# An adaLN and mixture-of-experts kernel: four experts' rows go into cleared tables instead of being added in DRAM

## The reference, cut to what matters

```python
x = x + ga * causal_mean(layernorm(x) * (1 + ca) + sa)     # softmax of a causal mask: a running mean
h = layernorm(x) * (1 + cb) + sb                           # S rows of D
scores = softmax(h @ gate_weight.T).T                      # E x S
vals, idx = top_k(scores.reshape(-1), 2 * S)               # 8192 (expert, row) pairs over all experts
gate = zeros(E, S).at[expert, row].add(vals)
y = gelu(h @ W1[e] + b1[e]) @ W2[e] + b2[e]                # for the chosen rows of each expert
shared = gelu(h @ Ws1 + bs1) @ Ws2 + bs2                   # for all rows
out = x + gb * (sum over e of gate[e] * y[e] + shared)
```

## Time and profile before

| | |
|---|---|
| median of 3 runs | 344.6 us (342.89 to 345.53) |
| the profiled execution | 346.31 us |
| its span (first to last instruction) | 344.3 us |
| granted TensorE clock, mean | 0.909 of full speed |
| PE busy | 272.8 us (79%) |
| POOL busy | 209.4 us (61%) |
| DVE busy | 158.4 us (46%) |
| ACT busy | 139.1 us (40%) |
| mean DMA rate | 70 GB/s |

### The profile page before, as it was taken

The page is one execution under the profiler, slowest core; times in us unless marked ns, Lnnn a source line. Parts: engine busy times, 40 slices in busy tenths (PEclk is TensorE's granted clock), DMA queues, the critical chain, the costliest instruction groups (busy, mean ns, idle before and its releaser), DMA issues.

```text
span 344.3 us, 4085 instructions
## 1 busy us (share of the span) xinstructions
PE 272.8 (79%) x1033; PEld 144.6 (42%) x1033; DVE 158.4 (46%) x758; ACT 139.1 (40%) x238; POOL 209.4 (61%) x242
## 2 busy tenths in 40 slices
PE   5889778999998596878999999999975916777400
PEld 1757765343444253444454444444432303336200
DVE  2899865567655446363945556342222202211100
ACT  4659966354333312324444444445421302333100
POOL 5667841000037374463888888788888888788661
PEclk9999995899999988989999999999988785998955
DMA  7901220039102242221534353535343332233321
GB/s 207 340 8 33 61 64 0 30 99 224 1 13 84 65 118 61 75 76 53 100 37 104 40 100 41 108 31 101 41 102 40 46 38 32 47 47 39 37 23 12
DMA packets 26463, 23.93 MB, mean 70 GB/s; under 512 B 7224, under 2 KB 21375, under 8 KB 26432
## 3 DMA queue, kind: packets, MB, share of 16 engines
q0 software_dynamic: 11968, 9.23, 19.8%
q1 hardware_dynamic: 14338, 14.32, 14.6%
q10 hardware_dynamic: 126, 0.04, 0.0%
HBM read 14.23 MB, written 9.34 MB: 68 GB/s over the span
## 4 chain that ended last, share of the span: by engine, by line
POOL 43%; issue 20%; PE 19%; DMA 6%; DVE 5%; ACT 2%; POOLq 1%; DVEq 1%; SPq 0%
POOL out_dram L1092 27%; POOL R L1074 15%; PE U L1236 6%; PE Y L1278 5%; DMA out_dram<-YO,IDXB 5%; PE Y L1167 2%; PE R L1125 1%; DVE YO L923 1%; PE LG L1188 1%; DVE ST L560 1%; DMA XW<-in_L_attn_x_dram 1%; ACT H2F L400 1%; PE U L1125 1%; PE R1b L1125 1%; DVEq L920 1%
## 5 line engine op out<-in xcount | busy, mean ns | idle before, releaser
L1092 POOL DMA_INDIRECT out_dram<-YO,IDXB x68 | 107.6, 1583 | 30.5 <-issue 22.3
L1074 POOL DMA_INDIRECT R<-rows_scratch,IDXB x68 | 66.3, 975 | 74.6 <-DVE IDXB L879 55.1
L464 ACT ACTIVATE HF<-U,COL 128x512 f32<-128x512 f32 x96 | 65.9, 687 | 102.6 <-PE U L1243 45.4
L1243 PE MATMUL U<-XT,XW 128*128 128x512 f32 x128 | 69.0, 630 | 2.9 <-issue 2.9
L1282 PE MATMUL Y<-HF,XW 128*128 128x512 f32 x128 | 66.4, 611 | 0.0
L923 DVE SCALAR_TENSOR_TENSOR YO<-R1b,R,GBR 128x128 f32<-128x128 f32 x64 | 18.0, 344 | 92.3 <-DMA out_dram<-YO,IDXB 50.3
L1236 PE MATMUL U<-H2F,WS 128*128 128x512 f32 x64 | 38.9, 693 | 0.1
L1243 PEld LDWEIGHTS U<-XT,XW 128*128 128x128 f32 x128 | 24.6, 204 | 29.2 <-issue 25.8
L1278 PE MATMUL Y<-HF,WS 128*128 128x512 f32 x64 | 35.9, 644 | 0.0
L1282 PEld LDWEIGHTS Y<-HF,XW 128*128 128x128 f32 x128 | 23.0, 195 | 19.8 <-issue 19.8
L485 ACT ACTIVATE XT<-R 128x512 f32<-128x512 f32 x17 | 10.2, 597 | 41.8 <-PE R L1125 40.3
(11 more groups left out here) (214 smaller groups left out, 351.6 us busy)
## 6 DMA issues: line engine op xcount, KB each, us to landing
XW<-in_wx_dram SPq DMA_DIRECT2D x10, 512.0 KB, 5.6
XW<-in_L_attn_x_dram SPq DMA_DIRECT2D x8, 256.0 KB, 7.4
rows_scratch<-HT SPq DMA_DIRECT2D x8, 256.0 KB, 3.3
out_dram<-SHO SPq DMA_DIRECT2D x8, 256.0 KB
R<-rows_scratch,IDXB POOLq DMA_INDIRECT x68
out_dram<-YO,IDXB POOLq DMA_INDIRECT x68
INV<-in_inv_dram SPq DMA_DIRECT2D x3, 256.0 KB, 6.8
WS<-in_wsx_dram SPq DMA_DIRECT2D x1, 512.0 KB, 6.8
```

The source lines that it names most:

```text
L464: eng.activation(HF[:, g % RING, :], UB[g % 2][:, :], ACT.Gelu_apprx_tanh, bias=B1[:, at:at + 1]).then_inc(M["a_gelu"], 1)
L1074: eng.indirect_dma_start(XG[:, v % XR, s, :], None, rows_dram, bass.IndirectOffsetOnAxis(ap=IDXB[:, v, s:s + 1], axis=0)).then_inc(M[f"ld_ ...
L1092: eng.indirect_dma_start(out, bass.IndirectOffsetOnAxis(ap=IDXB[:, v, s:s + 1], axis=0), YO[:, v % 2, s, :], None, compute_op=ALU.add).the ...
L1243: eng.matmul(bank[:, :], weights(v, 0, c, 0), XT[:, v % 2, :], start=True, stop=True).then_inc(M["pe_up"], 1)
```

## The change

Experts 0 to 3 (NTAB = 4, units 0 to 7) no longer add to the output. Each has a table of its own in DRAM (`sums`, S + 512 rows of 128). SP clears the tables with 16 DMAs of 512 KB (`clear`), 5 of them between the stores of the normalised rows and 11 behind the store of the scores. The eight scatters of units 0 to 7 write to these tables without adding and without waiting for each other.

The shared part stays in SBUF, in `X2`: `close` adds in place and nothing is stored then. When both units of an expert e have landed, SP loads its table back in eight pieces of 256 KB (`load_sums`) through four buffers, `TB`, which take the place of `INV`. DVE adds each piece to `X2` (`add_sums`): four at c = 1 and four at c = 2 of unit 2e+5, so in units 5, 7, 9 and 11. Pieces 4 to 7 can be loaded only when the adds of pieces 0 to 3 have freed a buffer. After the last expert's adds SP stores the eight blocks (`store_base`); scatter 8 waits for these stores, and scatters 8 to 16 add as before.

`YO` gets four buffers, `XG` twelve in place of ten. `gathered` lets GpSimd issue all that is left of the gathers behind scatter 7: with 50 issued by then, 18 follow in one run.

```diff
-XR = 10
+XR = 12
+NTAB = 4
+YR = 4
+TBR = 4
@@ def gathered(v):
-    return min(max(NT * AHEAD + PER_GAP * (v + 1), NT * (v + 4)), NT * NMAIN)
+    if v >= 2 * NTAB - 1:
+        return NT * NMAIN
+    return max(NT * AHEAD + PER_GAP * (v + 1), NT * (v + 4))
@@
+    sums = [nc.dram_tensor(f"sums_scratch{e}", [S + NPAD, D], F32, kind="Internal").ap() for e in range(NTAB)]
+        TB = INV
-        SHO = sb("SHO", [P, 2, BLK])
-        YO = sb("YO", [P, 2, NT, P])
+        YO = sb("YO", [P, YR, NT, P])
@@ def sync(eng):
+            def clear(i):
+                e, q = i // NT, i % NT
+                n = NB * NT // NT
+                eng.dma_start(by_partition(sums[e])[:, q * n:(q + 1) * n, :].rearrange("p (a t) c -> p a (t c)", t=NT),
+                              ZERO[:, :].unsqueeze(1).to_broadcast([P, n // NT, BLK])).then_inc(M["st_tz"], 16)
+
+            def load_sums(e, b):
+                if b == 0:
+                    for v in (2 * e, 2 * e + 1):
+                        eng.wait_ge(M[f"st_sc{v % YR}"], 64 * (v // YR + 1))
+                if NB * e + b >= TBR:
+                    eng.wait_ge(M["v_add"], NB * e + b - TBR + 1)
+                else:
+                    eng.wait_ge(M["v_ct"], NB)
+                eng.dma_start(TB[:, b % TBR, :].rearrange("p (t c) -> p t c", t=NT),
+                              by_partition(sums[e])[:, b * NT:(b + 1) * NT, :]).then_inc(M[f"ld_tb{b % TBR}"], 16)
+
+            def store_base(b):
+                eng.wait_ge(M["v_add"], NB * (NTAB - 1) + b + 1)
+                eng.dma_start(by_partition(out)[:, b * NT:(b + 1) * NT, :],
+                              X2[:, b, :].rearrange("p (t c) -> p t c", t=NT)).then_inc(M["st_out"], 16)
+
             for b in range(NB):
                 eng.wait_ge(M["a_ht"], b + 1)
                 eng.dma_start(by_partition(rows_dram)[:, b * NT:(b + 1) * NT, 0:D],
                               HT[:, b % NHT, :].rearrange("p (t c) -> p t c", t=NT)).then_inc(M[f"st_ht{b % NHT}"], 16)
+                if b < NB - 3:
+                    clear(b)
@@
+            for i in range(NB - 3, NTAB * NT):
+                clear(i)
             for s in range(NSTEP):
-                if s in CLOSE_AT:
-                    b = CLOSE_AT[s]
-                    eng.wait_ge(M["v_out"], b + 1)
-                    eng.dma_start(by_partition(out)[:, b * NT:(b + 1) * NT, :],
-                                  SHO[:, b % 2, :].rearrange("p (t c) -> p t c",
-                                                             t=NT)).then_inc(M[f"st_out{b % 2}"], 16)
@@
+                if c == 3 and v >= 4 and v % 2 == 0 and v // 2 - 2 < NTAB:
+                    for b in range(TBR):
+                        load_sums(v // 2 - 2, b)
+                if c == 0 and v >= 5 and v % 2 and v // 2 - 2 < NTAB:
+                    for b in range(TBR, NB):
+                        load_sums(v // 2 - 2, b)
+                if c == 3 and v == 2 * NTAB + 3:
+                    for b in range(NB):
+                        store_base(b)
@@ def vector(eng):
-                if b >= 2:
-                    eng.wait_ge(M[f"st_out{b % 2}"], 16 * (b // 2))
-                eng.tensor_tensor(SHO[:, b % 2, :], RB[1][:, :], X2[:, b, :], ALU.add).then_inc(M["v_out"], 1)
+                eng.tensor_tensor(X2[:, b, :], RB[1][:, :], X2[:, b, :], ALU.add).then_inc(M["v_out"], 1)
+
+            def add_sums(e, b):
+                eng.wait_ge(M[f"ld_tb{b % TBR}"], 16 * (NB // TBR * e + b // TBR + 1))
+                if e:
+                    eng.wait_ge(M["v_add"], NB * (e - 1) + b + 1)
+                else:
+                    eng.wait_ge(M["v_out"], b + 1)
+                eng.tensor_tensor(X2[:, b, :], TB[:, b % TBR, :], X2[:, b, :], ALU.add).then_inc(M["v_add"], 1)
@@ yo(v)
-                if v >= 2:
-                    eng.wait_ge(M[f"st_sc{k}"], 64 * (v // 2))
+                if v >= YR:
+                    eng.wait_ge(M[f"st_sc{v % YR}"], 64 * (v // YR))
@@ the steps
                 v, c = unit_step(s)
+                if v >= 5 and v % 2 and v // 2 - 2 < NTAB and c in (1, 2):
+                    for b in range((c - 1) * TBR, c * TBR):
+                        add_sums(v // 2 - 2, b)
@@ def gpsimd(eng):
             def scatter(v):
                 eng.wait_ge(M["v_yo"], v + 1)
-                if v == 0:
-                    eng.wait_ge(M["st_out0"], 16 * (NB // 2))
-                    eng.wait_ge(M["st_out1"], 16 * (NB // 2))
+                if v < 2 * NTAB:
+                    if v == 0:
+                        eng.wait_ge(M["st_tz"], 16 * NTAB * NT)
+                    for s in range(NT):
+                        eng.indirect_dma_start(
+                            sums[v // 2], bass.IndirectOffsetOnAxis(ap=IDXB[:, v, s:s + 1], axis=0),
+                            YO[:, v % YR, s, :], None).then_inc(M[f"st_sc{v % YR}"], 16)
+                    return
+                if v == 2 * NTAB:
+                    eng.wait_ge(M["st_out"], 16 * NB)
                 elif v >= NS or v % 2 == 0:
                     landed(v - 2)
                     landed(v - 1)
```

More of the change, by code:

```diff
@@ L75, in gathered @@
 def gathered(v):
-    return min(max(NT * AHEAD + PER_GAP * (v + 1), NT * (v + 4)), NT * NMAIN)
+    if v >= 2 * NTAB - 1:
+        return NT * NMAIN
+    return max(NT * AHEAD + PER_GAP * (v + 1), NT * (v + 4))
 SEMS = """ld_cst ld_uc ld_few ld_rows ld_x0 ld_x1 ld_x2 ld_x3 ld_x4 ld_x5 ld_x6 ld_x7 ld_wmod ld_ws ld_irow ld_inv1 ld_inv
 ld_wu0 ld_wu1 ld_wu2 ld_wu3 ld_xg0 ld_xg1 ld_xg2 ld_xg3 ld_xg4 ld_xg5 ld_xg6 ld_xg7 ld_xg8 ld_xg9
-st_z st_ht0 st_ht1 st_ht2 st_sc st_out0 st_out1 st_sc0 st_sc1
+ld_tb0 ld_tb1 ld_tb2 ld_tb3 ld_xg10 ld_xg11
+st_z st_tz st_ht0 st_ht1 st_ht2 st_sc st_out st_sc0 st_sc1 st_sc2 st_sc3
 pe_inv pe_few pe_cols pe_mod pe_gbc pe_cbr pe_t1 pe_t3 pe_t4 pe_t6 pe_lg pe_up pe_dn pe_out pe_sum pe_tie pe_cum pe_dq
@@ L86 @@
 a_dqo a_sil a_dg a_gbd a_gbc a_rat a_cbr a_xn a_xn2 a_h2f a_ht a_exp a_gelu a_sh a_dq a_xh a_ye
-v_ov v_sto v_few v_cols v_mod v_st v_ag1 v_ag2 v_xn v_xn2 v_ct v_x2 v_sub v_sc v_tk v_cnt v_cand v_mask v_kr v_tie v_sel v_out
+v_add v_ov v_sto v_few v_cols v_mod v_st v_ag1 v_ag2 v_xn v_xn2 v_ct v_x2 v_sub v_sc v_tk v_cnt v_cand v_mask v_kr v_tie v_sel v_out
 v_ds v_dq v_stc v_two v_flip v_eid v_oh v_used v_hm v_idx v_ix v_gread v_cb1 v_cb2 v_gt v_yo v_zero
@@ L918, in yo @@
                 eng.wait_ge(M["pe_yt"], v + 1)
-                if v >= 2:
-                    eng.wait_ge(M[f"st_sc{k}"], 64 * (v // 2))
+                if v >= YR:
+                    eng.wait_ge(M[f"st_sc{v % YR}"], 64 * (v // YR))
                 for t in range(NT):
                     gate = XG[:, r, t, D + v // 2:D + v // 2 + 1] if v < NS else GT4[:, k, t:t + 1]
-                    m = eng.scalar_tensor_tensor(YO[:, k, t, :], RB[1][:, t * P:(t + 1) * P], gate,
+                    m = eng.scalar_tensor_tensor(YO[:, v % YR, t, :], RB[1][:, t * P:(t + 1) * P], gate,
                                                  GBR[:, t, :], ALU.mult, ALU.mult)
@@ L1078, in landed @@
             def landed(v, tiles=NT):
-                eng.wait_ge(M[f"st_sc{v % 2}"], 64 * (v // 2) + 16 * tiles)
+                eng.wait_ge(M[f"st_sc{v % YR}"], 64 * (v // YR) + 16 * tiles)
             def scatter(v):
                 eng.wait_ge(M["v_yo"], v + 1)
-                if v == 0:
-                    eng.wait_ge(M["st_out0"], 16 * (NB // 2))
-                    eng.wait_ge(M["st_out1"], 16 * (NB // 2))
+                if v < 2 * NTAB:
[8 more added lines that the diff above has]
+                    eng.wait_ge(M["st_out"], 16 * NB)
                 elif v >= NS or v % 2 == 0:
@@ L1092, in scatter @@
                     eng.indirect_dma_start(
-                        out, bass.IndirectOffsetOnAxis(ap=IDXB[:, v, s:s + 1], axis=0), YO[:, v % 2, s, :], None,
-                        compute_op=ALU.add).then_inc(M[f"st_sc{v % 2}"], 16)
+                        out, bass.IndirectOffsetOnAxis(ap=IDXB[:, v, s:s + 1], axis=0), YO[:, v % YR, s, :], None,
+                        compute_op=ALU.add).then_inc(M[f"st_sc{v % YR}"], 16)
             def pair(v):
```

## The result

On the first chip the changed kernel took 362.5 us at the median of four executions (354.5 to 377.3), against 343.8 before: ratio 1.034 (95% interval 1.024 to 1.043, from its two faster executions; the two others, one of them the profiled one, lie more than 1.5% above the fastest). I had forecast 342.5, so the time is outside my range and on the other side. On three other chips the same kernel, with 328 to 329 us before at the median, gave 1.011 (1.006 to 1.016), 1.008 (1.003 to 1.012) and 1.005 (1.001 to 1.010). On 344.6 us these ratios would be 346 to 348, inside my range of 336 to 352, but slower and not faster. So there are two things to explain: a loss of 0.5 to 1.1% that the kernel carries with it, where I had said 0.6% faster, and over 2% more on the first chip, which is the larger part of the miss.

A forecast was written before the change was run, and what follows sets the result against it. GpSimd was taken to bound the kernel, TensorE 1.7 us a unit behind. Scatter 8 at 254.7, plus 79.9 and 7.6, gave a span of 342.2 against 344.3; median 342.5 us, range 336 to 352.

The forecast's parts named there:

- Plain scatters: Units 0 to 7: each takes the gather's price, 0.95 us, in place of 1.55 with adding.
- The kind of loss: Masks of units 14 and 16 come late from VectorE; two stands of TensorE with clock loss cost 4.9 us.
- with 3.3 us that lands at 196.9 and add 7 ends at 197.5: Unit 5: piece 7, issued at 193.5, lands in 3.3 us like a 256 KB store, and the last add follows.
- my 6.7: Unit 5, repeated in unit 7: eight adds hold VectorE for 6.7 us, 1.8 of them waiting.
- the stands of TensorE: At the masks of units 14 and 16: TensorE waits 1.7 us for each.
- where I had 4.9: Ahead of scatter 7: two stands of 1.7 us plus 0.75 for the clock each, 4.9 us together.
- the clock: After each stand TensorE may run at half rate: 0.75 us entered, with ends 0 and 1.5.
- my last rival: Adds and gathers exclude each other: 16 adds in the run of 18 gathers cost 9.8 us, median 352.3; chance 0.04.
- a gather that ran beside four `GBR` at 0.95 us: Gathers beside and clear of `GBR` both took 0.95 us, so the sum has no contention between VectorE and GpSimd.
- the base: Ahead of scatter 8: its store lands at 252.1, 2.6 us before GpSimd is free at 254.7.
- my second rival: Table pieces land later than 3.3 us: over 1% slower from 4.3 us, median 351.6 at 5.2 us; chance 0.17.
- The prediction's account of the tail: Behind scatter 8's start: 79.9 in place of 92.5 us, 16 gathers gone (20.5), three more gaps showing (9.1).

The follow-up runs named there:

- e4: Only the eight plain scatters of units 0 to 7 put into the kernel before, without clears, adds or table loads: 0.963, 314.7 us.
- e5: The kernel before, unedited, profiled on another chip: 1.003, span 326.9 us.
- e8: Only the 16 clears added to the kernel before: 1.000 of its time.
- e7: The changed kernel with eight table buffers and loads asked for earlier, adds still in groups of four: 0.980 of the kernel before, 322.3 us.
- e1_again: The changed kernel, unedited, on a second chip: 1.011 of the kernel before, 331.7 us.
- e13_again3: The changed kernel, unedited, on a fourth chip: 1.005 of the kernel before, 331.9 us.
- e3: The changed kernel without the 32 table loads, same adds made from what lies in the buffers: 0.982 of the kernel before, 321.5 us.
- e14: The changed kernel with every table piece loaded twice, first into a buffer nobody reads: 1.068 of the kernel before, 351.5 us.
- e9: The changed kernel with eight buffers, early loads, spread adds, and six gathers moved from the run of 18 into later gaps: 0.974 of the kernel before, 319.8 us.
- e2: The changed kernel with gathers paced as before, two behind a scatter: 1.054 of the kernel before.
- e11: The changed kernel, unedited, run a third time on another chip: 1.008 of the kernel before, 332.1 us.
- e12: The changed kernel with four buffers, only pieces 0 to 3 of each table asked for two units earlier: 1.001 of the kernel before.

## Why the prediction was wrong

**What held.** GpSimd was the bound before, with TensorE 1.7 us behind (e4, e5). Plain scatters cost nearly what a gather does where no adds run beside them. The clears cost nothing (e8), and eight adds take 4.9 us (e7). There are four gaps in the tail, and it is 86 to 87.5 us long. The kind of loss was foreseen as well: VectorE late with a mask, TensorE standing, GpSimd idle behind it.

**The step that failed** is "with 3.3 us that lands at 196.9 and add 7 ends at 197.5": the landing of a table piece. I took the median of the stores of rows. The first four pieces are asked for in one burst of 1 MB, behind 512 KB of weights and beside scatters and gathers, the others as buffers come free, and they took 4.1 us at the median and up to 6.1. In e1_again a group became 8.2 and 7.2 us for my 6.7, and the stands of TensorE 3.06 and 2.01 us for 1.7 (2.66 and 2.64 in e13_again3). That the waits for pieces are the loss is shown from three sides: without the loads (e3) or with the same loads asked for in time (e7) the stands are gone and the kernel is 2.5 to 3% faster, and with longer waits (e14) it is 6% slower.

**The terms beside it.** Ahead of scatter 7 TensorE lost 9.7 us in e1_again (three units in 34.9 us, from the turn at 178.40 to the one at 213.26, for 25.2), where I had 4.9. The stands are some 2 us of the difference; the larger part is the clock, 4.3 us for both stands where I had entered 1.5. In e13_again3 the clock costs 1.3 in sum, because it falls after only one of the stands. So that term changes from one execution to the next, while the stands are too long in both. Together scatter 7 came 3.7 and 1.7 us later than forecast.

Between scatters 7 and 8 are 3.1 us more than forecast in e1_again. Of them 1.4 lie in GpSimd's own transfers, which end at 242.7, and 1.7 in the wait for the base. e3, which waits for no load and no store there, is 2.0 us over the forecast by its transfers alone. Most of it is the contention that I had left out, my last rival in small: the adds were to cost GpSimd 9.8 us there, and cost at most 1.4 and 2.0. My argument was a gather that ran beside four `GBR` at 0.95 us; the 128x512 adds in an unbroken group do more (e7). As for the base, in e1_again its last add ends 8.7 us after `yo(9)`, where I had 6.4, and its stores land 5.2 us after issue at the median, up to 6.0, where I had 3.3 again.

It is my second rival, to which I gave 0.17. It was worked out as more than 1% slower from 4.3 us on; by its own sum 4.1 us gives 347.2, a ratio of 1.008, and the kernel is 0.5 to 1.1% slower. That this fits so well is in part luck, since its price of the clock was too low in e1_again and the contention was missing. The prediction's account of the tail doesn't close either: 20.5 us of gathers gone less 9.1 of new gaps are 11.4, and the tail was made 12.6 shorter.

I should have seen which way the error lay. Both rows of 256 KB transfers were before me, 3.3 and, in a queue, 7.4, and a burst of four behind weights is more like the queue.

**The first chip.** The above explains some 4 to 6 us of a miss of 20 (362.5 against 342.5). For the rest there is one profile. It is of the execution of 367.1 us; of the two that the ratio of 1.034 rests on, 357.9 and 354.5 us, there is none. It shows ScalarE, and then the busy time from 250 to 260 us (PE, PEld, DVE, ACT, POOL; then clock, DMA share, GB/s):

```profile
247.92 0.69 ACT L502 ACTIVATE HF<-U,COL 128x512 f32<-128x512 f32 x1 [5.06 <-issue]
255.68 0.69 ACT L502 ACTIVATE HF<-U,COL 128x512 f32<-128x512 f32 x1 [7.07 <-remote]
```

```profile
250.00:260.00 10.00, 0.26 (x1) 0.00 (x0) 0.00 (x0) 0.78 (x2) 7.57 (x8) 0.50 0.22 56
```

TensorE's turns for units 8 and 9 are 22.2 us apart (238.49 and 260.65) in place of 7.9; `yo(9)`, the last group of adds and the base are late by as much, and GpSimd stands 18.4 us ahead of scatter 8. Scatter 7 is also 5.4 us later after scatter 0 than in e1_again (73.9 us). The clock is at its lower level, but half rate would make 16 us of 7.9. TensorE has one matmul in these 10 us while ScalarE works on results of two, so some records are missing, and what TensorE waits for is not in the trace. The kernel before has stands on that chip too, four of 2.1 to 3.1 us between 112 and 149, where e5 has none of over 1 us; its scatter 0 comes at 162.1 against 145.4. Behind scatter 0 TensorE is ahead of GpSimd there, and nothing of the kind shows in the time. I think that the change took away this cover: in units 0 to 11 what TensorE loses now moves scatter 8. That would fit the spread (352 to 375 us of span against about 330 elsewhere), but no later run was on a chip of that level, so it is argued and not shown. Why TensorE stood there, and with it most of that chip's loss of 3.4%, stays open.

## What to carry to other kernels

A transfer's price is that of its place: take the landing of a transfer from a row with the same company (burst, weights ahead, other queues busy), not from a quiet stretch. If a load waits for the buffer that its own consumer frees, its landing is waited for again with each round of the ring: in e14 VectorE waited at every one of eight pieces. Ask for the data earlier and give it all the buffers, and nobody waits, though it lands no sooner (e7, 2.5 to 3% from the change as made).

Moving a bound from one engine to the next one 1.7 us behind it removes that engine's slack: a stand of over 2 us there now counts, and so does the half rate that often follows it. An argument that two engines don't disturb each other holds for the operations that it was read from: four small factors beside a gather said nothing of eight large adds beside a scatter.

A wait of fixed length on an in-order queue (the landing gaps) is a place for work that has to be done anyway: two gathers in each were free (e9).

## What the runs showed of the hardware

An indirect scatter of 128 rows of 512 bytes costs GpSimd 0.96 to 1.00 us without adding (e7, clear of VectorE's adds) and 1.56 with adding (e1_again). Beside an unbroken group of 128x512 float32 adds of two SBUF tiles on VectorE a plain one takes 1.34 to 1.50 us, and a gather between 0.94 and 1.52 (e7); the eight adds take their 4.89 us all the same. The adding scatters land 3.3 us after issue at the median, up to 5.0 (e1_again). Loads of 256 KB land in 2.8 to 6.1 us, median 4.1, when four are asked for at once and four singly (e1_again); in 2.7 to 8.6, median 5.7, when eight are asked for at once (e7); and at a median of 5.9 with twice the number (e14). TensorE went on at 2.4 GHz after 0.67 us idle. In the six profiles with stands at the masks of units 14 and 16 (e1_again, e2, e11, e12, e13, e14) the clock was at 1.2 GHz after ten stands of 2.01 to 8.02 us, and stayed at 2.4 GHz after two, of 2.64 and 2.93 us. Four chips agree on the kernel before within 0.5% (327.6 to 329.1 us); the first took 344, and nearly all of the difference lies ahead of the first scatter (e5).
